# Mixing stage with five chunks in flight, key squares on ScalarE, zero rows in the attention stacks

## The reference, cut to what matters

```python
x = x + attn_a(layernorm(x))      # 4 x 1024 tokens, 256 wide, 16 heads of 16; own layer norm, residual, softmax
x = x + ffn(layernorm(x))         # 256 x 256, weight rounded to -1, 0, 1 times a scale
x = x + attn_b(layernorm(x))      # memory layer, below
x = x + ffn(layernorm(x))

# attn_b(hidden):
k, v, q = (causal_conv4(hidden @ W.T, cw, cb) for the three)        # 64 wide
alpha = (sigmoid(hidden @ aW.T + ab) * 0.1).mean(-1)
eta = (sigmoid(hidden @ eW.T + eb) * 0.9 + 0.05).mean(-1)
theta = (softplus(hidden @ tW.T + tb) * 0.1).mean(-1)
for chunk of 128 tokens:
    g = 0.1 * grad of |silu(k W1.T) W2.T - v|^2, norm clipped to 1
    S = eta * S - theta * g ;  W = (1 - alpha) * W + S       # token by token
    retrieved = silu(q W1.T) W2.T
out = rmsnorm(retrieved @ Wo.T) * norm_g * (hidden @ gW.T + gb)
```

## Time and profile before

| | us |
|---|---|
| median of three runs | 1291.52 (1280.7 to 1293.97) |
| the profiled execution | 1291.08 |
| its span | 1289.1 |
| `attend`, first product to last output copy | 109.6 to 794.2 |
| `mix`, first product to first load of the next stage | 796.7 to 1048.85 |

### The profile page before, as it was taken

The page is one execution under the profiler, slowest core; times in us unless marked ns, Lnnn a source line. Parts: engine busy times, 40 slices in busy tenths (PEclk is TensorE's granted clock), DMA queues, the critical chain, the costliest instruction groups (busy, mean ns, idle before and its releaser), DMA issues. The chain is left out here.

```text
span 1289.1 us, 21939 instructions
## 1 busy us (share of the span) xinstructions
PE 1141.3 (89%) x8482; PEld 611.0 (47%) x8482; DVE 1021.7 (79%) x1634; ACT 794.3 (62%) x1562; POOL 210.4 (16%) x278
## 2 busy tenths in 40 slices
PE   6997899999999999999999997688888847789874
PEld 3663333333333333333333333466666537778763
DVE  5657799999999999999999981368888863477673
ACT  3550388888888888888888885264445612232320
POOL 4206000000000000000000001122322113354430
PEclk9997599999999999999999998799999867999996
DMA  8881312444134431343313002112331262223310
GB/s 278 202 288 66 51 34 45 68 60 65 34 49 68 60 60 35 52 68 61 57 40 56 19 18 88 63 46 90 107 120 58 99 174 69 75 70 89 101 34 33
DMA packets 87316, 101.55 MB, mean 79 GB/s; under 512 B 21868, under 2 KB 57196, under 8 KB 87212
## 3 DMA queue, kind: packets, MB, share of 16 engines
q1 hardware_dynamic: 86380, 98.56, 31.8%
q10 hardware_dynamic: 832, 1.58, 0.3%
HBM read 55.09 MB, written 43.88 MB: 77 GB/s over the span
## 5 line engine op out<-in xcount | busy, mean ns | idle before, releaser
L566 ACT ACTIVATE prob<-ps_s 128x512 f32<-128x512 f32 x1024 | 555.8, 597 | 121.2 <-PE ps_s L636 104.2
L587 DVE TENSOR_REDUCE maxes<-ps_m 128x2 f32<-128x1024 f32 x512 | 607.6, 1219 | 22.7 <-PE ps_m L625 18.8
L648 PE MATMUL ps_o<-prob,v_ones 128*32 128x256 f32 x4096 | 330.9, 395 | 7.8 <-issue 7.2
L636 PE MATMUL ps_s<-q_stack,k_stack 50*128 50x512 f32 x1024 | 263.8, 504 | 0.0
L625 PE MATMUL ps_m<-k_stack,q_stack 48*128 48x512 f32 x1024 | 220.8, 424 | 13.7 <-DVE maxes L587 11.0
L636 PEld LDWEIGHTS ps_s<-q_stack,k_stack 50*128 50x128 f32 x1024 | 100.4, 185 | 214.2 <-ACT prob L566 189.1
L648 PEld LDWEIGHTS ps_o<-prob,v_ones 128*32 128x32 f32 x4096 | 81.9, 108 | 194.3 <-issue 103.7
L625 PEld LDWEIGHTS ps_m<-k_stack,q_stack 48*128 48x128 f32 x1024 | 102.2, 194 | 30.2 <-DVE maxes L587 23.0
L528 POOL COPY v_ones<-v_all 128x512 f32<-128x512 f32 x16 | 9.9, 617 | 537.7 <-PE ps_o L648 537.7
L378 PE MATMUL ps_qk<-p_hT,p_wq 128*128 128x512 f32 x128 | 59.2, 618 | 1.7 <-ACT p_hT L329 1.7
L346 ACT ACTIVATE p_parts<-ps_qk,cols 128x512 fp32r<-128x512 f32 x32 | 22.0, 687 | 40.1 <-PE ps_qk L378 40.1
(11 more groups left out here) (200 smaller groups left out, 1459.1 us busy)
## 6 DMA issues: line engine op xcount, KB each, us to landing
qk_parts<-p_parts SPq DMA_DIRECT2D x32, 512.0 KB, 4.4
q_stack<-qk_parts SPq DMA_DIRECT2D x96, 128.0 KB, 4.6
k_stack<-qk_parts SPq DMA_DIRECT2D x96, 128.0 KB, 7.7
oT<-o_sb SPq DMA_DIRECT2D x32, 256.0 KB, 4.3
x_all<-in_x_dram SPq DMA_DIRECT2D x8, 512.0 KB, 10.0
heads<-oT SPq DMA_DIRECT2D x16, 256.0 KB
inverse<-inverse_sums SPq DMA_DIRECT2D x16, 256.0 KB
out_dram<-x_all SPq DMA_DIRECT2D x8, 512.0 KB, 3.8
```

The source lines that it names most:

```text
L566: act.activation(prob[at % P_RING][:, h], ps_s[:, (GH * at + h) % S_RING], ACT.Exp, scale=HD ** -0.5).then_inc(exp_done, 1)
L587: dve.tensor_reduce(maxes[:, i // 2, i % 2], ps_m[:, i % M_PAIRS], AX.X, ALU.max).then_inc(m_taken, 1)
L636: pe.matmul(ps_s[:, (GH * (UNITS * slot + KT * qc + kt) + h) % S_RING], r32(k_st[slot][rows, pair, kt * P:(kt + 1) * P]), r32(q_st[slot][r ...
L648: ins = pe.matmul(ps_o[32 * h:32 * h + 32, queries], v_st[slot][:, kt, h], prob[(UNITS * slot + KT * qc + kt) % P_RING][:, h, queries], st ...
```

## The change

In the stacks, rows 48 to 61 of each half are zeros in q and in k, and the two rows for maxima and ones move to 62 and 63: `MROW` is 62 and `ROWS` 64. Twelve transfers on SyncE's queue fill them, from a tile of zeros that GpSimd sets earlier; they stand between the ones and the first store.

In `mix` the iterations run from -4. The steps of z (add_out, put_z, turn_z, copy_zT) are one chunk further ahead (`it+3`), so are the out products (`it+4`) and the loads and divisions (`it+5`); the feed-forward stays at `it+2` and now uses the zT of the iteration before, of which there are two. TensorE's feed-forward products stand right behind the projections, turn_z behind the means. VectorE does two taps before put_z, the feed-forward adds before the decay scans, hid between the two groups of scans. x plus attention is written into `x_all`; `x1` is gone. The squares of the keys and their sums are made by ScalarE with a Square of the scaled key. The relu is written to the lower half of `sig_t`, and a column with 1/64 above and -1/64 below takes both means in one product. The division waits for the first half of the feed-forward products, and GpSimd's products no longer wait for hid.

```diff
-MROW = PAIRS * HD
-ROWS = MROW + 2
+DATA_ROWS = PAIRS * HD
+ROWS = P // 2
+MROW = ROWS - 2
...
+            sp.wait_ge(consts, 13)
+            for stack in stacks["q"] + stacks["k"]:
+                for base in BASES:
+                    sp.dma_start(stack[base + DATA_ROWS:base + MROW].rearrange("p h (n t) -> p (h n) t", t=P),
+                                 const["zeros"][0:MROW - DATA_ROWS].unsqueeze(1).to_broadcast([MROW - DATA_ROWS, HP * T // P, P])).then_inc(ones_placed, 16)
...
-            sp.wait_ge(ones_placed, 16 * 2 * SLOTS)
+            sp.wait_ge(ones_placed, 16 * 2 * SLOTS * 3)
...
+            made.did(pool.memset(const["zeros"][:], 0.0))
...
+            made.did(pool.memset(const["signed_mean"][HI], -1.0 / HALF))
+            made.settle()
...
-        x1, hT = two("x1", [P, TPC, C]), two("hT", [P, CH, CHUNK])
-        z, hid, zT = sb("z", [P, TPC, C]), sb("hid", [P, TPC, C]), sb("zT", [P, CH, CHUNK])
+        hT, zT = two("hT", [P, CH, CHUNK]), two("zT", [P, CH, CHUNK])
+        z, hid = sb("z", [P, TPC, C]), sb("hid", [P, TPC, C])
...
-        ITERATIONS = range(-3, NCH)
+        ITERATIONS = range(-4, NCH)
+
+        def x_of(n, lo=0, hi=TPC):
+            return x_all[:, TPC * n + lo:TPC * n + hi]
...
-                if it + 4 > 1 and valid(it + 4):
-                    load(it + 4)
+                if it + 5 > 1 and valid(it + 5):
+                    load(it + 5)
...
             for it in ITERATIONS:
-                if valid(it + 2):
-                    deviation(it + 2, 0, var_z, rstd_z)
-                if it + 4 > 1 and valid(it + 4):
-                    if valid(it):
-                        pool.wait_ge(conv, 2 * it + 2)
-                    divide_heads(pool, heads, it + 4)
+                if valid(it + 3):
+                    deviation(it + 3, 0, var_z, rstd_z)
+                if it + 5 > 1 and valid(it + 5):
+                    if valid(it + 2):
+                        pool.wait_ge(f_ready, 2 * (it + 2) + 1)
+                    divide_heads(pool, heads, it + 5)
                 if valid(it + 2):
                     deviation(it + 2, 1, var_h, rstd_h)
                 if valid(it):
-                    if valid(it + 2):
-                        pool.wait_ge(h_ready, it + 3)
                     memory_terms(it)
...
-                act.activation(relu_t[HI], ps_p[HI, 1], ACT.Relu, bias=theta_b)
+                act.activation(sig_t[LO], ps_p[HI, 1], ACT.Relu, bias=theta_b)
...
                 act.activation(kT[:], kv[:, 0], ACT.Copy).then_inc(kv_taken, 1)
+                act.wait_ge(kv_taken, n + 1)
+                for i in range(TPC):
+                    act.activation(squares[:, i], kT[:, i], ACT.Square, scale=0.2,
+                                   accum_out=small[s][:, i, SMALL_K2:SMALL_K2 + 1]).then_inc(k2_ready, 1)
...
-                act.activation(zT[:], ps_t[:], ACT.Copy).then_inc(zT_ready, 1)
+                if n > 1:
+                    act.wait_ge(f_ready, 2 * (n - 2) + 2)
+                act.activation(zT[n % 2][:], ps_t[:], ACT.Copy).then_inc(zT_ready, 1)
...
                     project_copies(it + 1)
-                if valid(it + 2):
-                    copy_zT(it + 2)
                 if valid(it + 1):
                     oldest_taps(it + 1)
                     log_sigmoid(it + 1)
                     means(it + 1)
+                if valid(it + 3):
+                    copy_zT(it + 3)
                 if valid(it):
                     keys_values(it)
...
             def add_out(n):
                 for k in range(2):
                     dve.wait_ge(w_ready, 2 * n + k + 1)
-                    dve.tensor_tensor(x1[n % 2][:, 2 * k:2 * k + 2], x_all[:, TPC * n + 2 * k:TPC * n + 2 * k + 2], ps_a[:, k],
-                                      ALU.add).then_inc(x1_ready, 1)
+                    dve.tensor_tensor(x_of(n, 2 * k, 2 * k + 2), x_of(n, 2 * k, 2 * k + 2), ps_a[:, k], ALU.add).then_inc(x1_ready, 1)
                 dve.wait_ge(x1_ready, 2 * n + 2)
-                moments(dve, steps_z, x1[n % 2], stats[:, n % 2, 0], mv[:, n % 2, 0], var_z, passed)
+                moments(dve, steps_z, x_of(n), stats[:, n % 2, 0], mv[:, n % 2, 0], var_z, passed)
...
             def add_ffn(n):
+                dve.wait_ge(z_ready, n + 1)
                 for k in range(2):
                     dve.wait_ge(f_ready, 2 * n + k + 1)
-                    dve.tensor_tensor(x_all[:, TPC * n + 2 * k:TPC * n + 2 * k + 2], x1[n % 2][:, 2 * k:2 * k + 2], ps_a[:, k], ALU.add).then_inc(x2_ready, 1)
+                    dve.tensor_tensor(x_of(n, 2 * k, 2 * k + 2), x_of(n, 2 * k, 2 * k + 2), ps_a[:, k], ALU.add).then_inc(x2_ready, 1)
                 dve.wait_ge(x2_ready, 2 * n + 2)
-                moments(dve, steps_h, x_all[:, TPC * n:TPC * (n + 1)], stats[:, n % 2, 1], mv[:, n % 2, 1], var_h, passed)
+                moments(dve, steps_h, x_of(n), stats[:, n % 2, 1], mv[:, n % 2, 1], var_h, passed)
...
-                dve.wait_ge(kv_taken, n + 1)
-                if n:
-                    dve.wait_ge(k2_ready, TPC * n)
-                for i in range(TPC):
-                    dve.tensor_tensor_reduce(squares[:, i], kT[:, i], kT[:, i], 0.04, 0.0, ALU.mult, ALU.add,
-                                             small[s][:, i, SMALL_K2:SMALL_K2 + 1]).then_inc(k2_ready, 1)
...
-                if valid(it + 2):
-                    add_out(it + 2)
+                if valid(it + 3):
+                    add_out(it + 3)
                 if valid(it):
                     tap(it, 1)
-                if valid(it + 2):
-                    put_z(it + 2)
+                    tap(it, 2)
+                if valid(it + 3):
+                    put_z(it + 3)
                 if valid(it):
-                    tap(it, 2)
                     tap(it, 3)
-                    scan_decays(it)
                 if valid(it + 2):
                     add_ffn(it + 2)
                 if valid(it):
-                    scan_keeps(it)
+                    scan_decays(it)
                 if valid(it + 2):
                     put_h(it + 2)
                 if valid(it):
+                    scan_keeps(it)
                     products_of_keys(it)
...
             def out_products(n):
                 pe.wait_ge(heads["divided"], n + 1)
                 for k in range(2):
-                    if n > 1:
-                        pe.wait_ge(gate_taken, 2 * (n - 2) + k + 1)
+                    if valid(n - 3):
+                        pe.wait_ge(gate_taken, 2 * (n - 3) + k + 1)
+                    elif valid(n - 2):
+                        pe.wait_ge(x2_ready, 2 * (n - 2) + k + 1)
                     elif n:
-                        pe.wait_ge(x2_ready, k + 1)
+                        pe.wait_ge(x1_ready, 2 * (n - 1) + k + 1)
                     token_products(k, o[n % 2], w_out, w_ready)
 
             def ffn_products(n):
                 pe.wait_ge(zT_ready, n + 1)
                 for k in range(2):
-                    pe.wait_ge(x1_ready, 2 * n + k + 1)
-                    token_products(k, zT, w_t, f_ready)
+                    if valid(n + 1):
+                        pe.wait_ge(x1_ready, 2 * (n + 1) + k + 1)
+                    else:
+                        pe.wait_ge(gate_taken, 2 * (n - 2) + k + 1)
+                    token_products(k, zT[n % 2], w_t, f_ready)
...
             def turn_z(n):
                 pe.wait_ge(z_ready, n + 1)
-                if n:
-                    pe.wait_ge(hT_ready, n)
+                if n > 1:
+                    pe.wait_ge(hT_ready, n - 1)
+                elif n:
+                    pe.wait_ge(zT_ready, n)
                 turn(z, zT_turned)
 
             def turn_h(n):
                 pe.wait_ge(h_ready, n + 1)
-                pe.wait_ge(zT_ready, n + 1)
+                if valid(n + 1):
+                    pe.wait_ge(zT_ready, n + 2)
+                else:
+                    pe.wait_ge(hT_ready, n)
                 turn(hid, hT_turned)
...
-                    pe.matmul(ps_p[:, 1, i:i + 1], relu_t[HI, c], const["mean"][HI, 0:1], start=True, stop=False)
-                    ins = pe.matmul(ps_p[:, 1, i:i + 1], sig_t[HI, c], const["minus_mean"][HI], start=False, stop=True)
+                    ins = pe.matmul(ps_p[:, 1, i:i + 1], sig_t[:, c], const["signed_mean"][:], start=True, stop=True)
...
                 if valid(it + 2):
-                    turn_z(it + 2)
+                    ffn_products(it + 2)
                 if valid(it + 1):
                     gate_means(it + 1)
-                if valid(it + 2):
-                    ffn_products(it + 2)
+                if valid(it + 3):
+                    turn_z(it + 3)
                 if valid(it):
                     key_products(it)
                 if valid(it + 1):
...
                     theta(it + 1)
                 if valid(it + 2):
                     turn_h(it + 2)
-                if valid(it + 3):
-                    out_products(it + 3)
```

(2 more changed lines are left out.)

14 lines of the change are left out of this document (7 added, 7 removed).

## The result

The changed kernel took 1243.91 us in the median of its runs (1243.31 to 1248.13); the kernel before 1289.57 in the same comparison. The ratio is 0.9667, with a 95% interval of 0.9632 to 0.9702. Whether that is B's doing or a coincidence is what the comparison by stage has to show.

The account below looks back on a forecast made before the run. It took the mixing stage to be bound by a chain of waits round through TensorE and VectorE, VectorE the fuller. 1291.1 +2.5 (prologue) -33.2 (full iterations) -7.4 (tail) gave 1253 us; own range 1247 to 1261, 8 in 10 within 1241 to 1269.

Parts of the forecast that it names:

- B: Rival: TensorE's clock in the attention rises earlier, at 139 instead of 160 us; -9.3 us, time 1244, chance 0.27.
- Full iterations: Mixing stage: four iterations at 21.8 us and a fifth without out products, 106.7 against 139.9, so -33.2 us.
- The walk: One mixing iteration timed step by step from the projections: TensorE done at 21.8 us, hid at 16.3, needed 17.3.
- Squares, hidden: Mixing stage: key squares leave VectorE (2.2 us a chunk) and are hidden on ScalarE, 1.07 us for four.
- Theta, -0.9 a chunk: Mixing stage: half of the 16 one-column theta products go, saving 0.9 us of TensorE per chunk.
- The division's stall, 0: Mixing stage: GpSimd's moved division stalls no VectorE scan, 0 us; upper bound 0.7 in each of three iterations.
- Prologue: Start of the mixing stage: one iteration more, second projections at 853.9 to 856 instead of 852.1, +2.5 us.
- Tail: End of the mixing stage: 49.4 us instead of 56.8, so -7.4 us.
- The zero-transfers, forecast 0: First stage: twelve more transfers take 5 to 9 us of SyncE's queue, cost 0; at most 4 if backlog isn't absorbed.
- C: Rival: in mixing iterations the low clock stays and the lock lands on taps or scans; 1270 us, chance 0.18.
- D: Rival: no gain, a late step (hid or second out add) keeps the mixing period near 26; 1285 us, chance 0.06.
- E: Rival: slower, the attention's stack products cost by rows, +97 us; 1350 us, chance 0.04.

Follow-up runs that it names:

- old_order: The kernel before with only the key squares moved to ScalarE and one theta product per tile, four chunks in flight; 1286.51 us, ratio 0.9941.
- theta_twice: The changed kernel with each theta product issued twice, the second overwriting the first with the same value; 1251.15 us, ratio 0.9671.
- division_on_scans: The changed kernel with GpSimd's division held back until the second moments are through, so beside the decay scans; 1255.65 us, ratio 0.9705.
- mix_only: The changed kernel without its zero rows and their transfers, stacks of 48 and 50 rows again; 1250.98 us, ratio 0.9692.
- zeros_only: The kernel before with the zero rows and their transfers alone added; 1284.99 us, ratio 0.9962.
- zeros_memset: The changed kernel with the zero rows made by six memsets on VectorE and GpSimd instead of twelve transfers; 1242.85 us, run again 1243.22.

## Why the prediction was right, and where not

**What bounds the kernel.** "A chain that goes round through both": right. old_order shows it best, since work taken out beside the chain changed nothing. "With VectorE the fuller" said nothing of the bound. VectorE's own work was put at 20.4 us and is 19.88: the sum took its idle time as 2.1, where its row leaves 2.66 (26.80 less 24.14).

**Full iterations, forecast -33.2, measured -36.4** (849.56 to 953.07, 103.5; 104.5 in the second profile). The walk is right step for step: feed-forward products end at 8.7, gates at 15.9 (16.3 forecast), hid at 16.2 (16.3), keeps at 19.4 (19.5), G at 20.0 (20.1). The period is 21.03 instead of 21.8 because the turn of z, the gates, theta and the turn of h each take 0.1 to 0.2 us less than their terms in the walk, and the other steps together 0.2. The lead of hid was put at 1.0 and is 0.43: since TensorE is faster, it also asks sooner.

**Squares, hidden: right.** Four squares and their reads take 1.07 us on ScalarE (885.49 to 886.56), no table load comes with them. That they "go" from VectorE as a gain is only true in the new order.

**Theta, -0.9 a chunk: right** in the new order (theta_twice, 0.90), worth nothing in the old one.

**The division's stall, 0: wrong, by little.** "No scan over 0.5 us under the division" was the sign, and 17 of 21 divisions in the seven profiles stretch one. The walk took the division to lie beside adds and moments, but its load lands so late that it mostly ends on the first scan. In the first profile this costs 0.53 us, in the second 0.72 and 0.80. The upper bound of 0.7 per iteration was mis-sized too: division_on_scans gives up to 3.3. It subtracted the spare time of the whole period from the stall, but what counts is the lead of the late step at its place, and in two of three iterations TensorE's clock fell behind the wait.

**Prologue, forecast +2.5, measured +1.7** (57.07 against 55.37). Right in size.

**Tail, forecast -7.4, measured -5.7.** The last hid ends 16.3 into its iteration, as said. From there to the end it is 34.8 instead of 33.1. A step was left out. With the squares gone, the taps of the last two chunks come right behind G and so beside GpSimd's products:

```profile
986.02 1.39 DVE L1011 SCALAR_TENSOR_TENSOR p_kv_c<-p_pre_kv,cols,p_kv_c 128x512 f32<-128x512 f32 x1
987.33 1.10 DVE L1011 SCALAR_TENSOR_TENSOR p_q_c<-p_pre_q,cols,p_q_c 64x512 f32<-64x512 f32 x1
...
990.15 0.75 DVE L1011 SCALAR_TENSOR_TENSOR p_kv_c<-p_pre_kv,cols,p_kv_c 128x512 f32<-128x512 f32 x1
```

They have two SBUF inputs; the first three take 1.3 us more than their like, for each of these two chunks, so 2.5 together. The way from the start of the last G to the end is 0.7 shorter than before (5.85 against 6.52), which leaves about the 1.7 that the tail is longer than forecast. Before, the squares lay there and took the stretch on themselves (0.91 in the earlier trace rows), and the tap behind them took its 0.74.

**The zero-transfers, forecast 0: wrong.** They take 16.4 us of the queue, not 5 to 9. The estimate took the price of a transfer of 2 rows for one of 14 (0.73 us for one of the ones; 1.23 and 1.50 for one of zeros), and then called the rest absorbed because the first store "is needed by ScalarE at 42". It is the whole backlog that is late: ScalarE waits for stores from 42 to 85 us, and the first stage grows by 2.7 (2.8 in the mean of eight profiles with the transfers, 110.07 to 112.42, against six without, 108.16 to 109.58). The bound of 4 for that case held.

**The attention: the likeliest case was wrong, rival B happened**, with -7.0 instead of -9.3. B's place was too early (139; the level rose at 149) and that the rows have to do with the level is what mix_only, zeros_only and the two profiles of zeros_memset speak for; how they do it stays open. Its time of 1244 agrees with the measured one, but not because the sum was right elsewhere: 1253 plus 2.7 in the first stage, less 7.0 in the attention, 2.3 in `mix` and 1.9 in the memory stage. Of these only the 2.7 and the 7.0 have a cause in the change that was missed. The second profile of the changed kernel has `mix` at 214.0, which is the forecast, and the median of the seven is 213.5; but that, too, is a sum of misses that cancel (in the second profile the prologue is 1.2 and the full iterations 2.2 shorter than forecast, the tail 3.4 longer). The memory stage, whose code isn't edited, scatters from 237.6 to 240.8 in the profiles, so the 1.9 can't be told from scatter. Without the earlier rise the time would be an estimated 1251 (1243.9 plus 7.0), within the forecast's own 1247 to 1261; that it fell below these is B's doing.

**Rivals C, D and E fell.** C: the granted clock in full iterations is 1.00. Its lower level is real, though, and shows when a wait comes back (two of three iterations of division_on_scans). D: the period is 21.03. E: 48 and 62 rows both take 401 ns.

**Left open.** Why zero rows bring TensorE's level up sooner, why old_order rose after four rounds without them, and whether rows filled with other values do the same. The last wasn't tried.

## What to carry to other kernels

Before counting what an edit takes off an engine, find the round of waits and ask whether the work lies on it: beside the round the gain turns into a longer wait, and a longer wait can bring TensorE's lower clock with it and cost more than it saved. So break the round first, then trim the engine that is full. When an operation is moved out of another's way, ask what sets its start: here it was a load, and its landing decided how much of the old conflict was left. Count small filling transfers in a shared queue one by one and follow the whole backlog, not the first item behind them; if an engine stands idle at the start, let it write the constants.

## What the runs showed of the hardware that was not expected

- In the attention's head TensorE is busy 5.00 of 5 us at a granted clock of 0.50, and how long it stays so went with how many rows the products contract, zeros among them: 9, 9 and 4 rounds with 48 and 50 rows, 3 with 48 and 64, 1 or 2 in ten profiles with 62 and 64, worth 0.92 us a round. In the one profile with more products in the 25 us ahead of it the rise did not come sooner.
- A wait of 1.5 us in an otherwise full TensorE was followed by a transpose of 1.83 instead of 1.07 us and out products of 4.60 instead of 3.62, but not each time: one period later the same wait (1.48) was followed by 1.09 and 3.62.
- Six broadcasts of 14 rows out of a 512-byte source row took 7.38 and 9.00 us in SyncE's queue (112 KB each), while a memset of a whole stack (128 x 2048) took 1.80 us on GpSimd and 1.76 on VectorE.
